# A graph network on one core: a reordered attention loop, and zeros written in an earlier stage

## The chip, the core and the metric

The kernel runs on one core of a Trainium2 chip. The metric is device time in microseconds. The core has a matrix engine (PE, with its weight loads shown as PEld), a vector engine (DVE), an activation engine (ACT), a general engine (POOL, which also starts the indirect DMAs), and SP, whose queue starts the plain DMAs. The engines run side by side and meet only in semaphores.

## What is computed

Four layers over a graph of 3125 nodes with 128 features and 103125 edges, sorted by destination. Before each layer x is normalized and passed through a relu, and each layer's result is added to x.

```python
edge_index = jnp.stack([src, dst])
x = x + gcn(relu(layernorm(x)), edge_index)          # counts of edges and degrees, two linear steps, softmax
x = x + additive_attention(relu(layernorm(x)))       # 4 heads: exp(tanh(xs + xd) . att), weighted sums
x = x + gat(relu(layernorm(x)))                      # 2 heads, below
x = x + interaction(relu(layernorm(x)), edge_attr)   # below

# gat
xl = (h @ Wl + bl).reshape(n, H, D); xr = (h @ Wr + br).reshape(n, H, D)
e = leaky_relu(xl[src] + xr[dst], 0.2)
alpha = segment_softmax(einsum('ehd,hd->eh', e, att), dst)
out = segment_sum(xl[src] * alpha[..., None], dst).mean(axis=1)

# interaction
msg = (rbf @ k2f_W) * (xa @ Wj + bj)[idx_j]
xj = segment_sum(msg, idx_i)                         # idx_i = src: not sorted
```

## The kernel before

The edges are cut into 202 tiles of 512 (four blocks of 128). Since they are sorted by destination, the destinations of a tile lie in a window of 20 nodes. The kernel is a chain of stages. Each stage is a block in which every engine has a program of its own, and the next stage begins when all engines are through.

**The degree count** (`count_degrees`, L769 on, stage "deg") comes early, in the first layer. DVE writes the two digits of each destination as one-hot rows, 101 steps of two instructions (L790), PE counts with them, ACT and DVE make the inverse root, and SP stores the result and loads it back in two forms (L842 to L848). POOL has nothing to do in it.

**The attention loops** (`attend`, L1321 on) serve both the additive layer and the GAT layer (`gat` is true). `over_tiles` writes out, for each engine, the order of its steps in one period, each step with a lag: `(3, scores)` means that in the period of tile s the scores of tile s-3 are made. A step's waits are semaphores counted by tile. For one period of the GAT loop, PE runs:

- `scores` (L1412, L1415): a matmul with the one-hots and four passes with the activated features, into bank 4, which has no second buffer;
- `turn_sums` (L1457): turns the sums of tile s-5, two transposes, into bank 7. It waits for ACT's `copy_sums` and until `best` holds all tiles up to s-4, since the best scores lie in bank 7 too;
- `features` (L1399, L1403): eight transposes of gathered rows and two matmuls with the window of the destinations;
- `sums` (L1443): eight passes over the gathered rows with the edge weights, into bank 6. It waits for `edge_weights`, and it is what releases POOL's next `gather` into the same slot, six tiles on;
- `turn` (L1424): four transposes of the exponentials; `turn_top` (L1434): the best scores per node into bank 7.

DVE runs `tops` (largest score, L1521 to L1528), `keep_sums` (L1548, takes turned sums out of bank 7), `onehots` (L1158), `leaky` (L1514), `edge_weights` (L1535, takes the turned exponentials out of bank 5) and `best_of_nodes` (L1541, L1544, reads bank 7). ACT runs `raise_scores` (the exponential, L1482), `activate` (L1474 in the GAT loop, L1476 in the additive one) and a copy of the sums (L1488, in the additive loop `keep_sums`, L1494). POOL gathers four blocks of source rows per tile (L744). SP loads indices, local rows and windows.

In the additive loop PE runs scores, features, turn, sums; scores and weights have two banks each there.

**The interaction layer** makes messages and adds them to eight tables in DRAM by indirect DMAs with an add (L1309), since its sums aren't sorted. The tables, `k.sums`, have to be zero. This is done in `load_sources` (L2079 on, stage "srcs"), right ahead of the loop's preparation: DVE clears half of `k.wide` and SP writes it to each of the eight tables with two DMAs, a large one and a small one:

```python
for two in k.sums:
    for table in two:
        sp.dma_start(table[0:k.n_nodes, :]..., zeros...).then_inc(zeroed, 16)
        sp.dma_start(table[k.n_nodes:k.n_nodes + P, :], zeros[:, 0:F]).then_inc(zeroed, 16)
```

The stage also loads the sources of all edges and casts them to float (L2094). Of the buffers, `k.fa` is half of `fm_ab`; in the degree count nobody else uses it.

Of the kernel before, what the change touches and what calls it, by code (L numbers as in the profile page):

```python
# [33 lines left out]
P = 128  # L34
F = 128
# [4 lines left out]
SUB = 4  # L40
TILE = P * SUB
RING = 4
DEEP = 6
# [725 lines left out]
def count_degrees(k):  # L769
# [23 lines left out]
    with Stage(k, "deg") as st:  # L793
        step, digits, high_ready, low_ready, counted = (st.sem("step"), st.sem("digits"), st.sem("high_ready"),
                                                        st.sem("low_ready"), st.sem("counted"))
        rooted, inverted, stored, spread = st.sem("rooted"), st.sem("inverted"), st.sem("stored"), st.sem("spread")
        with st.block() as block:
            @block.vector
            def _(dve):
# [39 lines left out]
            @block.sync  # L839
            def _(sp):  # L840
                sp.wait_ge(inverted, 1)
                sp.dma_start(k.isd.rearrange("(h l) -> h l", l=DIGIT), found).then_inc(stored, 16)  # L842
                sp.wait_ge(stored, 16)
                with nc.allow_non_contiguous_dma(reason="one number per node"):
                    sp.dma_start(k.inv_sqrt_deg[:, :], k.isd.rearrange("(o n) -> o n", o=1).to_broadcast(
                        [P, k.n_nodes])).then_inc(spread, 16)
                    sp.dma_start(k.inv_sqrt_deg_nm[:, :], k.isd.rearrange("(b p) -> p b", p=P)).then_inc(spread, 16)
                sp.wait_ge(spread, 32)  # L848


# [470 lines left out]
def attend(k, name, a, table, table_dst):  # L1321
# [33 lines left out]
    with Stage(k, name) as st:  # L1355
# [12 lines left out]
        with st.block() as block:  # L1368
# [20 lines left out]
            def _(pe):  # L1389
# [70 lines left out]
                if gat:  # L1460
                    over_tiles(pe, k.tiles, [(3, scores), (5, turn_sums), (1, features), (4, sums), (3, turn),
                                             (3, turn_top)], head=2, ring=DEEP)
                else:
                    over_tiles(pe, k.tiles, [(2, scores), (1, features), (3, turn), (4, sums)], head=2,
                               ring=DEEP)

            @block.scalar
            def _(act):
# [31 lines left out]
                else:  # L1500
                    over_tiles(act, k.tiles, [(2, raise_scores), (1, activate), (4, keep_sums)], head=2, ring=DEEP)

            @block.vector
            def _(dve):
# [46 lines left out]
                if gat:  # L1551
                    over_tiles(dve, k.tiles, [(3, tops), (5, keep_sums), (0, onehots), (1, leaky),
                                              (3, edge_weights), (3, best_of_nodes)], head=2, ring=DEEP)
                else:
# [524 lines left out]
def load_sources(k):  # L2079
# [4 lines left out]
    k.earlier = k.fb[:, 0:SUB * P].rearrange("p (j e) -> p j e", e=P)  # L2084
    zeros = k.wide[:, 0, :]
    with Stage(k, "srcs") as st:
        loaded, cleared, zeroed = st.sem("loaded"), st.sem("cleared"), st.sem("zeroed")
        with st.block() as block:
            @block.vector
            def _(dve):  # L2090
                dve.memset(zeros, 0.0).then_inc(cleared, 1)
                dve.tensor_scalar(k.spare[:, :], k.iota_p[:, :], float(k.n_nodes), None, ALU.add)
# [3 lines left out]
            @block.sync  # L2096
            def _(sp):
                sp.dma_start(raw, k.ins["src_edges"]).then_inc(loaded, 16)
                sp.wait_ge(cleared, 1)
                for two in k.sums:  # L2100
                    for table in two:
                        sp.dma_start(table[0:k.n_nodes, :].rearrange("(b p) f -> p b f", p=P),
                                     zeros.rearrange("p (b f) -> p b f", f=F)).then_inc(zeroed, 16)
                        sp.dma_start(table[k.n_nodes:k.n_nodes + P, :], zeros[:, 0:F]).then_inc(zeroed, 16)
                sp.wait_ge(loaded, 16)
                sp.wait_ge(zeroed, 32 * 2 * SUB)

# [138 lines left out]
```

## Time and profile before

| | us |
|---|---|
| median of 3 runs | 5661.89 (5657.54 to 5664.57) |
| the profiled execution | 5659.49 |
| its span, first to last instruction | 5657.8 |
| PE busy in the span | 3980.4 (70%) |
| POOL busy | 3127.6 (55%) |
| DVE busy | 2796.4 (49%) |
| ACT busy | 1440.7 (25%) |

The rows further down come from one profiled execution. Times are microseconds from the start of its span unless marked ns. An engine's busy time is the time in which it had an instruction running; the ends of matmuls are modelled, so that rows of PE are best read from start to start. The granted clock of PE is given in parts of 2.4 GHz. The DMA share is how busy the 16 DMA engines were on average. A row of the windows gives the stretch, its length, the busy time of each engine with its count of instructions, the granted clock, the DMA share and the GB/s. In brackets behind a row of a timeline stands how long its engine had been idle before, and what ended that; "issue" means that the profile shows nothing that it waited for.

### The profile page before, as it was taken

How to read it: one execution, taken by the hardware profiler on the slowest of the kernel's cores; microseconds unless marked ns; L12 is line 12 of the kernel's file. 1: busy time of each engine (PE TensorE's matmuls, PEld its weight loads, DVE VectorE, ACT ScalarE, POOL GpSimd, SP SyncE). 2: the span in 40 equal slices, each digit the busy share in tenths (PEclk: the TensorE clock that was granted, in tenths of full speed). 3: DMA queues.
4: the chain of work that ended last, by engine and by line, in shares of the span. 5: the costliest groups of instructions: out<-in, count | busy, mean ns of one | idle time of the engine just before them, and what ended most of it. 6: DMA issues, size and time to landing. Idle time of an engine off the chain costs nothing. (4 is left out here: it accounts for less than half of the span.)

```text
span 5657.8 us, 85234 instructions
## 1 busy us (share of the span) xinstructions
PE 3980.4 (70%) x18200; PEld 2339.9 (41%) x18200; DVE 2796.4 (49%) x7514; ACT 1440.7 (25%) x3414; POOL 3127.6 (55%) x3371
## 2 busy tenths in 40 slices
PE   3499564989888724999999999326666566656525
PEld 2233333555545412444444444015555555545401
DVE  7799123333333354555555555544444444444447
ACT  0233102333333212333333333011111111111125
POOL 0061123777777522555555554406888888888810
PEclk9999786887888756999999999565555555555557
DMA  1122332222222103333333332045566666666540
GB/s 31 34 67 88 97 96 69 69 70 69 69 69 69 41 0 97 99 97 97 98 97 97 97 97 75 1 114 100 94 96 97 95 97 96 97 96 96 88 100 12
DMA packets 515411, 447.78 MB, mean 79 GB/s; under 512 B 175623, under 2 KB 430678, under 8 KB 515030
## 3 DMA queue, kind: packets, MB, share of 16 engines
q0 software_dynamic: 180992, 211.97, 20.7%
q1 hardware_dynamic: 334294, 234.52, 15.2%
q14 instruction: 92, 0.75, 0.0%
q8 instruction: 33, 0.54, 0.0%
HBM read 336.65 MB, written 109.55 MB: 79 GB/s over the span
## 5 line engine op out<-in xcount | busy, mean ns | idle before, releaser
L1309 POOL DMA_INDIRECT sums<-gathered,idx x808 | 1307.3, 1618 | 419.0 <-issue 228.3
L744 POOL DMA_INDIRECT gathered<-table,idx x1088 | 1028.8, 946 | 796.8 <-DMA idx<-in_src_rows 285.2
L1415 PE MATMUL bank<-zact,att_cells 128*64 128x512 f32 (+1 forms) x1212 | 683.4, 676 | 0.9 <-ACT zact L1476 0.5
L744 POOL DMA_INDIRECT wide<-table,idx x528 | 498.8, 945 | 250.9 <-issue 135.7
L1235 PE MATMUL bank<-msg,gathered 128*128 128x128 f32 x1616 | 418.9, 441 | 262.6 <-DVE msg L1277 262.6
L1521 DVE TENSOR_REDUCE neg_raw<-bank 80x1 f32<-80x512 f32 (+1 forms) x404 | 276.5, 684 | 608.0 <-PE bank L1415 608.0
L1482 ACT ACTIVATE msg<-bank,neg_top 80x512 f32<-80x512 f32 (+1 forms) x404 | 275.9, 683 | 1121.2 <-DVE neg_top L1523 1116.2
L978 POOL TENSOR_TENSOR acc<-acc,msg 128x20 f32 x404 | 176.4, 437 | 617.9 <-issue 397.0
L1235 PEld LDWEIGHTS bank<-msg,gathered 128*128 128x128 f32 x1616 | 360.0, 328 | 315.7 <-DVE msg L1277 161.5
L1295 DVE TENSOR_TENSOR idx<-picked,partial 128x4 int32<-128x4 f32 x202 | 33.2, 164 | 803.3 <-DMA sums<-gathered,idx 802.3
L1217 PE MATMUL bank<-w_L_gnn_k2f_W,edge_rows 64*128 64x128 f32 x1616 | 418.9, 438 | 10.2 <-DMA edge_rows<-in_attr_rows 10.2
L1251 ACT COPY gathered<-bank 128x512 f32<-128x512 f32 x202 | 118.4, 586 | 1108.7 <-DMA sums<-gathered,idx 1101.4
L1217 PEld LDWEIGHTS bank<-w_L_gnn_k2f_W,edge_rows 64*128 64x128 f32 x1616 | 359.6, 325 | 55.6 <-issue 44.7
L1399 PE MATMUL bank<-ident,gathered 128*128 128x128 f32 x1632 | 292.1, 304 | 100.2 <-DMA gathered<-table,idx 98.8
L1225 PE MATMUL bank<-window,onehot_t 60*128 60x128 bf16 x808 | 121.3, 303 | 325.0 <-DVE onehot_t L1158 321.0
L1535 DVE COPY edge_rows<-bank 128x320 f32<-128x320 f32 (+1 forms) x404 | 185.2, 458 | 324.1 <-PE bank L1424 323.9
L1514 DVE TENSOR_TENSOR zact<-zact,bank 128x512 f32<-128x512 f32 x404 | 259.7, 684 | 149.4 <-ACT zact L1474 149.4
L1399 PEld LDWEIGHTS bank<-ident,gathered 128*128 128x128 f32 x1632 | 208.8, 152 | 266.4 <-issue 135.4
L927 DVE TENSOR_SCALAR gathered<-iota_c,partial 128x500 f16<-128x500 f16 x812 | 304.7, 391 | 3.3 <-issue 1.6
L1158 DVE TENSOR_SCALAR onehot_t<-dst_row,iota_w,always 64x512 bf16<-64x512 bf16 x606 | 264.5, 436 | 67.0 <-DMA dst_row<-local_rows 41.8
L1443 PE MATMUL bank<-gathered,edge_rows 128*64 128x256 f32 x1088 | 263.9, 385 | 0.0
L935 PE MATMUL bank<-gathered,zact 128*128 128x500 f16 x812 | 209.7, 381 | 69.9 <-DVE zact L928 59.4
(313 smaller groups left out, 6492.3 us busy)
## 6 DMA issues: line engine op xcount, KB each, us to landing
zact<-in_src_flat SPq DMA_DIRECT2D x202, 256.0 KB, 3.4
dst_row<-local_rows SPq DMA_DIRECT2D x606, 64.0 KB, 2.8
edge_rows<-in_attr_rows SPq DMA_DIRECT2D x202, 128.0 KB
gathered<-table,idx POOLq DMA_INDIRECT x1088, 2.7
sums<-gathered,idx POOLq DMA_INDIRECT x808, 3.5
sums<-wide SPq DMA_DIRECT2D x8, 1600.0 KB
counts<-wide SPq DMA_DIRECT2D x4, 3000.0 KB, 12.1
counts<-fm_ab SPq DMA_DIRECT2D x4, 3000.0 KB, 12.0
```

Of the source, the lines that this page charges most:

```text
L744: pool.indirect_dma_start(out=g[:, j, :], out_offset=None, in_=table, in_offset=bass.IndirectOffsetOnAxis(ap=k.idx[t.slot][:, j:j + 1], ax ...
L927: dve.tensor_scalar(k.cell_hot[slot][:, j, :], k.iota_c[:, :], k.cell[:, q], None, ALU.is_equal)
L1158: return dve.tensor_scalar(k.onehot_t[buf][:, :], k.dst_row[t.slot][:, :], k.iota_w[0:HROWS, 0:1], k.always[0:HROWS, 0:1], ALU.is_equal, A ...
L1217: mm = pe.matmul(k.bank[t.two][:, j * F:(j + 1) * F], k.attr[t.two][0:depth, j * P:(j + 1) * P], k.w["L3_gnn_k2f_W"][:, :], start=True, st ...
L1235: mm = pe.matmul(k.bank[4 + t.two][:, j * F:(j + 1) * F], same(t)[:, j, :], k.msg[t.two][:, j, :], start=True, stop=True)
L1309: pool.indirect_dma_start(out=k.sums[t.two][j], out_offset=bass.IndirectOffsetOnAxis(ap=k.idx[t.slot][:, j:j + 1], axis=0), in_=out_rows(t ...
L1399: pe.matmul(z_bank(t, h)[:, j * P:(j + 1) * P], g[:, j, h * F:(h + 1) * F], k.ident[:, :], is_transpose=True, start=(j == 0), stop=False, ...
L1415: mm = pe.matmul(score_bank(t), a.att[h][:, :], k.zact[t.two][:, h, :], start=False, stop=(h == a.zs - 1))
L1443: mm = pe.matmul(sum_bank(t), weights(t)[:, j, :], g[:, j, :], start=(j == 0), stop=(j == SUB - 1))
L1482: act.activation(raised(t), score_bank(t), ACT.Exp, bias=k.neg_top[0:cells, bass.ds(t.t, 1)], accum_out=k.weight_sum[0:cells, bass.ds(t.t, ...
L1514: m = dve.tensor_tensor(za, za, z_bank(t, h)[:, :], ALU.max)
L1521: dve.tensor_reduce(raw, score_bank(t), AX.X, ALU.max, negate=True).then_inc(top_found, 1)
```

## The change

- In the GAT loop PE's order becomes scores, features, turn_sums, sums, turn_top, turn: turn_sums goes behind features, and turn_top ahead of turn.
- In the GAT loop DVE's order becomes tops, onehots, keep_sums, leaky, best_of_nodes, edge_weights.
- In the additive loop ACT runs activate ahead of raise_scores.
- The zeros of the eight tables are written in the degree count: POOL clears `k.fa`, SP issues the 16 DMAs from there, ahead of its other work in the stage, and waits for them at the stage's end. In "srcs" DVE's memset, the 16 DMAs and their wait are gone.

```diff
@@ count_degrees @@
+        cleared, zeroed = st.sem("cleared"), st.sem("zeroed")
         with st.block() as block:
+            @block.gpsimd
+            def _(pool):
+                pool.memset(k.fa[:, :], 0.0).then_inc(cleared, 1)
...
             @block.sync
             def _(sp):
+                sp.wait_ge(cleared, 1)
+                for two in k.sums:
+                    for table in two:
+                        sp.dma_start(table[0:k.n_nodes, :].rearrange("(b p) f -> p b f", p=P),
+                                     k.fa[:, :].rearrange("p (b f) -> p b f", f=F)).then_inc(zeroed, 16)
+                        sp.dma_start(table[k.n_nodes:k.n_nodes + P, :], k.fa[:, 0:F]).then_inc(zeroed, 16)
                 sp.wait_ge(inverted, 1)
...
                 sp.wait_ge(spread, 32)
+                sp.wait_ge(zeroed, 32 * 2 * SUB)
@@ attend @@
-                    over_tiles(pe, k.tiles, [(3, scores), (5, turn_sums), (1, features), (4, sums), (3, turn),
-                                             (3, turn_top)], head=2, ring=DEEP)
+                    over_tiles(pe, k.tiles, [(3, scores), (1, features), (5, turn_sums), (4, sums), (3, turn_top),
+                                             (3, turn)], head=2, ring=DEEP)
...
-                    over_tiles(act, k.tiles, [(2, raise_scores), (1, activate), (4, keep_sums)], head=2, ring=DEEP)
+                    over_tiles(act, k.tiles, [(1, activate), (2, raise_scores), (4, keep_sums)], head=2, ring=DEEP)
...
-                    over_tiles(dve, k.tiles, [(3, tops), (5, keep_sums), (0, onehots), (1, leaky),
-                                              (3, edge_weights), (3, best_of_nodes)], head=2, ring=DEEP)
+                    over_tiles(dve, k.tiles, [(3, tops), (0, onehots), (5, keep_sums), (1, leaky),
+                                              (3, best_of_nodes), (3, edge_weights)], head=2, ring=DEEP)
@@ load_sources @@
-                dve.memset(zeros, 0.0).then_inc(cleared, 1)
...
-                sp.wait_ge(cleared, 1)
-                for two in k.sums:
-                    for table in two:
-                        sp.dma_start(table[0:k.n_nodes, :].rearrange("(b p) f -> p b f", p=P),
-                                     zeros.rearrange("p (b f) -> p b f", f=F)).then_inc(zeroed, 16)
-                        sp.dma_start(table[k.n_nodes:k.n_nodes + P, :], zeros[:, 0:F]).then_inc(zeroed, 16)
                 sp.wait_ge(loaded, 16)
-                sp.wait_ge(zeroed, 32 * 2 * SUB)
```

## Rows read from the trace of the kernel before

**Rows 1.** Windows, us: busy of PE, PEld, DVE, ACT, POOL; clock, DMA share.

```profile
2230.00:3530.00 1300.00, 1296.73 (x6248) 635.84 (x6249) 711.72 (x2017) 438.34 (x1009) 758.78 (x803) 1.00 0.35 96
945.00:1960.00 1015.00, 894.06 (x3994) 511.61 (x3992) 345.44 (x810) 394.28 (x1403) 742.83 (x786) 0.81 0.27 67
3830.00:5400.00 1570.00, 942.67 (x4040) 788.78 (x4040) 691.78 (x1616) 236.85 (x404) 1306.68 (x808) 0.50 0.60 95
53.00:164.00 111.00, 59.57 (x803) 48.04 (x804) 110.72 (x203) 0.00 (x0) 0.00 (x0) 1.00 0.00 0
3772.00:3818.00 46.00, 0.00 (x0) 0.00 (x0) 0.19 (x1) 0.00 (x0) 0.00 (x0) 0.50 0.94 280
```

**Rows 2.** Groups, additive loop, 1000 to 1900: busy us, mean ns | idle before, releaser.

```profile
L744 POOL DMA_INDIRECT gathered<-table,idx x480 | 453.8, 945 | 146.3 <-issue 131.0 <-PE bank L1447 15.2
```

**Rows 3.** Timeline, PE, one tile of the GAT loop: start, us, operation [idle before].

```profile
2806.64 0.46 PE L1424 MATMUL bank<-ident,msg 64*128 64x64 f32 x4
2807.03 0.20 PE L1434 MATMUL bank<-top_cells,own 64*2 64x20 f32 x2
2807.16 0.40 PE L1412 MATMUL bank<-onehot_t,far 64*64 64x512 bf16 x1
2807.49 1.93 PE L1415 MATMUL bank<-zact,att_cells 128*64 128x512 f32 x4
2809.35 0.33 PE L1457 MATMUL bank<-ident,tile_rows 64*128 64x64 f32 x2
2809.62 1.09 PE L1399 MATMUL bank<-ident,gathered 128*128 128x128 f32 x8
...
2811.17 1.94 PE L1443 MATMUL bank<-wide,edge_rows 128*64 128x256 f32 x8
2813.05 0.46 PE L1424 MATMUL bank<-ident,msg 64*128 64x64 f32 x4
```

**Rows 4.** Timeline of the stage srcs and the two after it, SP's queue and DVE.

```profile
3768.22 0.36 SPq L2098 DMA_DIRECT2D partial<-in_src_edges  x1
...
3771.62 0.57 DVE L2094 CAST partial<-partial 128x808 f32<-128x808 int32 x1
...
3822.08 0.06 DVE L517 MEMSET win_off<- 128x1 f32 x1 [49.89 <-PEq L158]
3822.93 0.33 DVE L429 TENSOR_SCALAR base<-first,win_off 128x202 f32<-128x202 f32 x1 [0.78 <-PEq L158]
```

**Rows 5.** Timeline of setup, POOL: a memset of 128 columns.

```profile
1.68 0.19 POOL L323 MEMSET ones<- 128x128 f32 x1
```

**Rows 6.** Line L1158 in the interaction loop, 3850 to 5300: count, ns min/median/max.

```profile
L1158 DVE TENSOR_SCALAR onehot_t<-dst_row,iota_w,always x190: 395/405/754, 3850.8 to 5296.3; 64x512 bf16<-64x512 bf16 x190
```

**Rows 7.** Timeline, GAT loop, the same tile: DVE and ACT.

```profile
2808.19 0.16 DVE L1544 TENSOR_TENSOR fm_ab<-fm_ab,bank 2x20 f32 x1
...
2810.56 0.68 ACT L1482 ACTIVATE msg<-bank,neg_top 64x512 f32<-64x512 f32 x1 [3.45 <-DVE neg_top L1523]
...
2810.68 0.28 DVE L1548 COPY partial<-bank 128x40 f32 x1
...
2811.91 1.28 DVE L1514 TENSOR_TENSOR zact<-zact,bank 128x512 f32<-128x512 f32 x2 [0.72 <-ACT zact L1474]
```

**Rows 8.** Timeline, PE, end of the GAT loop, where features have run out.

```profile
3520.49 0.33 PE L1457 MATMUL bank<-ident,tile_rows 64*128 64x64 f32 x2
3520.76 1.51 PE L1443 MATMUL bank<-gathered,edge_rows 128*64 128x256 f32 x6
```

**Rows 9.** Groups, GAT loop, 2300 to 3500, weight loads: busy us, mean ns | idle before.

```profile
L1443 PEld LDWEIGHTS bank<-gathered,edge_rows 128*64 128x64 f32 x1001 | 126.8, 136 | 112.2 <-issue 53.0
...
L1399 PEld LDWEIGHTS bank<-ident,gathered 128*128 128x128 f32 x1000 | 106.9, 141 | 8.5
...
L1424 PEld LDWEIGHTS bank<-ident,msg 64*128 64x128 f32 x752 | 60.9, 138 | 72.3 <-issue 72.3
...
L1434 PEld LDWEIGHTS bank<-top_cells,own 64*2 64x2 f32 x376 | 15.7, 79 | 12.7
```

More of the change, by code:

```diff
@@ L2084, in load_sources @@
     k.earlier = k.fb[:, 0:SUB * P].rearrange("p (j e) -> p j e", e=P)
-    zeros = k.wide[:, 0, :]
     with Stage(k, "srcs") as st:
-        loaded, cleared, zeroed = st.sem("loaded"), st.sem("cleared"), st.sem("zeroed")
+        loaded = st.sem("loaded")
         with st.block() as block:
```

## The prediction

> **What bounds the kernel now.** I first cut the span into its stages and read, for each, the busy time of every engine, the granted clock and the share of DMA [rows 1]. Three loops over the 202 tiles carry most of it. In the GAT loop (first row) PE is busy 1296.7 of 1300 us at a granted clock of 1.00, which is its 2.4 GHz level, and no other engine reaches 60%: it is bound by PE. In the additive loop (second row) PE is busy 88% at 0.81, which mixes 1.2 and 2.4 GHz; POOL has 742.8 us of 1015, but the row of its gathers shows that this is full [rows 2]: 945 ns busy and 0.30 us of idle before each (146.3/480), nearly all of it issue, so 1.25 us in all, and 4 x 1.25 = 5.0 us is the whole period of a tile (202 x 5.0 = 1010). That loop is bound by POOL. The interaction loop (third row) has POOL at 83%, with its scatters. The last two rows are stages between loops: while the degrees are counted the DMA queues carry nothing (share 0.00), with DVE busy all through; while the tables are zeroed the DMA share is 0.94 and no engine has work.
>
> Next I read one period of the GAT loop on PE [rows 3]. From start to start: turn 0.39, turn_top 0.13, first matmul of scores 0.33, the rest of scores 1.86, turn_sums 0.27, features 1.55, sums 1.88, together 6.41 us; 202 tiles make 1295 us. There is no idle row in between. Whatever the reorder does to waits can bring nothing here unless the work itself gets shorter.
>
> **Part 1, the zeros.** Removed from the stage "srcs": one memset, 16 DMAs and the wait for them. The stage now issues its load of the sources at 3768.22, casts at 3771.62 and hands over to the next stage at 3822.08 [rows 4]. Left over are the load and the cast. The cast began at 3771.62, so the load had landed by then; it takes 0.57, and from the end of one stage to the first instruction of the next DVE idles 0.78 (last row of the group). So the next stage starts at 3771.62 + 0.57 + 0.78 = 3772.97 instead of 3822.08: **-49.1 us**. Everything behind it is shifted, since the chain there is serial.
>
> Added to the degree count: a memset on POOL and the same 16 DMAs on SP's queue, then a last wait. The 16 transfers ran some 46 us at 280 GB/s [rows 1]; begun with the one-hots at about 54 they end near 100, even at half the rate near 146. The store of the degrees, which they stand in front of in SP's queue, is only due when DVE ends at 164. So they are hidden; uncovered they would cost the 46 us again. What isn't hidden is what they do to DVE, on which this stage hangs. The memset: POOL cleared 128 columns in 0.19 us [rows 5], so 3200 take at most 25 x 0.19 = 4.7 us. DVE's digit operations at the head of the stage run beside it; if they had to wait it out it would cost 4.7, if they don't meet, 0. The nearest row is a DVE tensor_scalar beside POOL's scatters and the busiest DMA of a loop (a share of 0.60) [rows 1, 6]: minimum 395, median 405, maximum 754 ns. The median is 2.5% over the minimum, so I take **+1 us** for memset and the 46 us of traffic together (2.5% of 46 is 1.2), with 0 and 4.7 + 1.2 = 6 as ends.
>
> The Trainium skill ("SBUF — State Buffer", section "SBUF: two separate sides") says that VectorE in a two-port mode and GpSimd take one port pair as an exclusive lock for a whole instruction. By it the digit operations would wait for the whole memset, and the sum would be some 4 us higher; the median of 405 beside POOL doesn't show it, the 754 ns maximum may.
>
> **Part 2, the additive loop.** ACT's activate of a new tile now goes ahead of the exponential of the one before. PE needs the activated tile for the scores of the next period, and the exponential only for turn, behind the next scores and features. Neither touches POOL, which issues without a pause. By the lags in the code PE makes the sums of tile s-4 when it takes the rows of s-1, and POOL waits for the sums six tiles back, so it stands some two tiles before its release. I take **0**. A gain is excluded by the 5.0 us of four gathers; a loss needs PE to fall two periods (10 us) behind.
>
> **Part 3, the GAT loop.** No instruction is added. PE runs scores, features, turn_sums, sums, turn_top, turn. Counting from the start of scores (2807.16) and keeping the lengths above, features starts at 2.19, turn_sums at 3.74, sums at 4.01, turn_top at 5.89, turn at 6.02, the next scores at 6.41. Each wait against that:
> - turn_sums needs the best scores of the tile before; DVE had them at 2808.19 + 0.16, which is 1.19 [rows 7], and gets them earlier now. Spare 2.5 us; before it was 1.0, the tightest of all.
> - turn_top needs keep_sums, 0.28 us on DVE behind turn_sums: 4.01 + 0.28 and an allowance of 0.1 make 4.4, against 5.89. Spare 1.5 us.
> - turn needs the exponential, done at 2810.56 + 0.68, so 4.08, against 6.02. Spare 1.9 us.
> - sums of the next period, at 10.4, needs edge_weights, which now stands behind best_of_nodes: it starts after turn (6.41), waits for at most 0.33 of best_of_nodes and ends before 7.4. Spare 3 us.
> - What is queued behind keep_sums on DVE is leaky; it started at 2811.91 (4.75), after ACT. keep_sums is through at 4.4. Should it come later, leaky has until the scores two periods on.
> - POOL's gathers are released by sums, which ends as before.
>
> So no wait opens, and PE stays full. What is open is whether a stage costs the same behind another neighbour. One new pair happens at the end of the loop already, where the features have run out: turn_sums straight into sums, 0.27 us from start to start [rows 8], as long as turn_sums into features. The other pairs I price from the loads. Bounds: each stage begins with a weight load (79 to 141 ns [rows 9]), and six neighbours change; every stage keeps its own load, so what can change is how much of it shows. I take **0** for the period; the ends are half a load of 138 ns saved a tile, and twice the 54 ns of rival 1 lost: -14 and +22 us. At the very end of the loop best_of_nodes comes before edge_weights, and the last turn_sums waits less: **-1 us**.
>
> **Sum.** The profiled execution took 5659.5 us (5657.8 of span and 1.7 around it), 2.4 below the median of 5661.9. 5659.5 - 49.1 + 1 + 0 + 0 - 1 = 5610.4, and at the median's level **5613 us** (-0.86%).
>
> **Rivals.**
> 1. *Exposed weight loads.* A load is hidden behind a long stage and bare behind a short one. Bare before: those of turn_top and features (79 + 141 ns); bare now: those of turn and sums (138 + 136), with the one of scores bare in both [rows 9]. That is +54 ns a tile, 202 x 0.054 = 11 us: 5624; with twice as much 5635. Against it: before the first load of turn the loader sat idle for 0.38 us a tile (72.3/188), behind the longest stage, so that load isn't pulled ahead and hidden now either. The Trainium skill ("TensorE: Matmul & The Clock Gate", section "Step-by-step: what each phase is for") says that PE pulls weight loads ahead of matmuls in flight; this rival is what that rule gives here.
> 2. *Cheaper neighbours.* The mirror image: turn_top's tiny load (79 ns) now follows the longest stage, and PE saves the 0.07 a tile of the lower end: 5599.
> 3. *The zeros hurt the degree count.* If its DVE work is held by the memset and slowed by traffic past my bound, by 15% over 46 us, it is 7 + 4 us in place of the 1: 5623. For it: no row shows DVE beside a DMA share of 0.94. Against it: the 2.5% at 0.60.
> 4. *Slower: a bubble that takes the clock down.* If PE has to wait in each period, for keep_sums behind turn_sums, it loses the wait and perhaps the 2.4 GHz too: the additive loop, where PE is idle 12% of the time, is granted 0.81. At 0.90 the GAT loop's 1297 us become 1441, 5757 in all. It decides from 0.24 us a tile (49/202). keep_sums would have to be 1.5 us later than I make it before PE waits at all.
> 5. *The zeros aren't taken off the path.* If SP's queue were still full of them when the degrees are due, part of the 49 us comes back in the degree count; the 60 us between 100 and 164 speak against it. With all of it back, 5662.
>
> **Chances.** Forecast (5606 to 5619) 0.58; rival 1 0.18; rival 2 0.11; rival 3 0.06; rival 4 0.04; rival 5 0.03. The range of **5598 to 5634** takes in the first four but for the worst of rival 1. About 0.2% (11 us) is what a measurement of this kernel can tell from no change. Faster by more than that: 0.93; within it: 0.03; slower: 0.04.
>
> **What would show it.** In the profile after, "srcs" should pass from its load to the next stage in about 5 us instead of 54, and the stretch of the degree count should show a DMA share near 0.9 for some 46 us, with DVE's one-hots at 0.54 us each (110.7/203) and the count ending within 1 to 6 us of before. The GAT loop should keep 6.41 us a tile at a clock of 1.00 with no idle time on PE; a period of 6.46 is rival 1, one of 6.34 rival 2, a clock under 1.00 with PE waiting for DVE rival 4. The additive loop should keep its 1.25 us a gather. I'm wrong if PE's period moves by more than 0.1 us, or if the one-hots get longer beside the zeros.

## The result, and the profile after

| | before | after |
|---|---|---|
| median, runs side by side | 5663.23 (5657.54 to 5666.03) | 5589.58 (5584.73 to 5596.26) |
| ratio, 95% interval | | 0.9872 [0.9855, 0.9889] |
| profiled execution / its span | 5659.5 / 5657.8 | 5584.7 / 5583.0 |
| PE busy | 3980.4 | 3953.5 |

The change saves 73.7 us, where 49 were forecast; 5589.6 lies below the range of 5598 to 5634. Lines have moved by 12 or so: of the kernel after, L1424 is the far matmul of scores, L1427 its four passes (here called att), L1411 and L1415 the transposes and the windows of features, L1469 turn_sums, L1455 sums, L1446 turn_top, L1436 turn.

One period of the GAT loop on PE, from the timeline of after (start, us, operation; it answers to rows 3):

```profile
2799.90 0.46 PE L1436 MATMUL bank<-ident,msg 64*128 64x64 f32 x4
2800.29 0.40 PE L1424 MATMUL bank<-onehot_t,far 64*64 64x512 bf16 x1
2800.62 1.93 PE L1427 MATMUL bank<-zact,att_cells 128*64 128x512 f32 x4
2802.48 1.09 PE L1411 MATMUL bank<-ident,gathered 128*128 128x128 f32 x8
2803.51 0.60 PE L1415 MATMUL bank<-onehot_t,window 60*128 60x512 bf16 x2
2803.95 0.28 PE L1469 MATMUL bank<-ident,tile_rows 64*128 64x64 f32 x2
2804.16 1.94 PE L1455 MATMUL bank<-wide,edge_rows 128*64 128x256 f32 x8
2806.03 0.20 PE L1446 MATMUL bank<-top_cells,own 64*2 64x20 f32 x2
2806.16 0.46 PE L1436 MATMUL bank<-ident,msg 64*128 64x64 f32 x4
```

The period is 2806.16 - 2799.90 = 6.26 us, where it was 6.41. Counted over some 1060 us it is 6.262 (169 tiles), before 6.407 (166 tiles). The same 30 instructions run, and two stretches of them are shorter. From start to start, the windows take 0.44 us, and turn_sums 0.21 (0.26 to 0.27 before). The windows took 0.53 before, as this row, the one left out of rows 3, shows (timeline of before; sums starts at 2804.77):

```profile
2804.24 0.60 PE L1403 MATMUL bank<-onehot_t,window 60*128 60x512 bf16 x2
2804.77 1.94 PE L1443 MATMUL bank<-gathered,edge_rows 128*64 128x256 f32 x8
```

All others are as long as they were [rows 3]. What happened between the two shows in the weight loads. First before, then after, in the timelines of PEld; in brackets stands how long the loader had been idle:

```profile
2809.35 0.20 PEld L1457 LDWEIGHTS bank<-ident,tile_rows 64*128 64x128 f32 x2 [0.81 <-issue]
...
2811.17 1.05 PEld L1443 LDWEIGHTS bank<-wide,edge_rows 128*64 128x64 f32 x6 [0.42 <-issue]
```

```profile
2802.48 0.86 PEld L1411 LDWEIGHTS bank<-ident,gathered 128*128 128x128 f32 x8 [0.81 <-issue]
2803.50 0.11 PEld L1415 LDWEIGHTS bank<-onehot_t,window 60*128 60x128 bf16 x2 [0.16 <-issue]
2803.73 0.35 PEld L1469 LDWEIGHTS bank<-ident,tile_rows 64*128 64x128 f32 x2
2804.15 1.49 PEld L1455 LDWEIGHTS bank<-wide,edge_rows 128*64 128x64 f32 x8
```

Set each load's start beside that of its first matmul. Before, the load of turn_sums starts at 2809.35 and so does its matmul [rows 3]: the load lies bare. After, it starts at 2803.73 and its matmul at 2803.95, while the second matmul of the windows is still running: it is hidden. Every other first load of a stage is bare in both kernels: taken as means from 2400 to 3360 us, all eight of before start 0.002 to 0.004 us ahead of their matmul, and so do seven of after, while the one of turn_sums starts 0.214 ahead. The two stretches together are 0.145 us shorter, about one load (0.137 us), and 202 times that is the 29 us.

The stages, as windows (stretch, length, busy of PE, PEld, DVE, ACT, POOL; clock, DMA share, GB/s), answering to rows 1:

```profile
2230.00:3500.00 1270.00, 1264.98 (x6227) 650.60 (x6228) 721.88 (x2009) 423.37 (x1006) 762.90 (x808) 0.99 0.36 99
945.00:1960.00 1015.00, 889.50 (x4005) 509.99 (x4005) 348.02 (x813) 384.67 (x1407) 744.38 (x789) 0.82 0.27 67
53.00:104.00 51.00, 25.57 (x344) 20.60 (x344) 50.86 (x94) 0.00 (x0) 0.00 (x0) 1.00 0.95 267
104.00:164.00 60.00, 32.70 (x440) 26.39 (x441) 60.00 (x112) 0.00 (x0) 0.00 (x0) 1.00 0.00 0
```

PE is still full in the GAT loop and the additive loop is as it was. The last two rows show the zeros: DMA share 0.95 up to 104, then nothing, with DVE full in both. The head of the degree count, in the timelines of DVE and POOL after:

```profile
50.17 3.15 DVE L806 TENSOR_SCALAR wide<-dst_f 128x808 f32<-128x808 f32 x1 [0.70 <-PEq L158]
...
50.13 2.76 POOL L801 MEMSET fm_ab<- 128x3200 f32 x1 [42.31 <-POOLq L158]
```

DVE's first digit operation takes 3.15 us beside POOL's memset; the same operation took 0.58 before:

```profile
50.46 0.58 DVE L801 TENSOR_SCALAR wide<-dst_f 128x808 f32<-128x808 f32 x1 [0.70 <-PEq L158]
```

And the stage srcs, with the two behind it (timeline of SP's queue and DVE, answering to rows 4):

```profile
3744.14 0.37 SPq L2108 DMA_DIRECT2D partial<-in_src_edges  x1
...
3747.39 0.58 DVE L2104 CAST partial<-partial 128x808 f32<-128x808 int32 x1 [3.04 <-DMA partial<-in_src_edges]
...
3749.55 0.33 DVE L429 TENSOR_SCALAR base<-first,win_off 128x202 f32<-128x202 f32 x1 [0.78 <-PEq L158]
```

**Where the 74.8 us between the two profiled executions are.** The first transpose of the GAT loop comes at 2226.43 before and 2231.98 after: +5.5. SP's store of the degrees went from 165.44 to 167.73, so 2.3 of that is the degree count. The other 3.2 is no more than executions differ by at that point: it came at 2232.95 in a kernel whose only edit lies behind it (e3). From that transpose to the last turn_sums: 1305.6 to 1276.2, **-29.4**. From there to the stage srcs: -0.2. From the load of the sources to L429: 54.7 to 5.4, **-49.3**. Behind that: -1.4.

### The profile page after: what moved, and what is told of

It is laid out like the page before. It is cut to its first block and busy times, and to the rows that moved or that the text cites. A ratio compares the mean times of both kernels' runs of the same rounds, so it can differ in the third digit from the quotient of the medians.

```text
span 5583.0 us, 85234 instructions
## 1 busy us (share of the span) xinstructions
PE 3953.5 (71%) x18200; PEld 2357.2 (42%) x18200; DVE 2813.4 (50%) x7513; ACT 1415.3 (25%) x3414; POOL 3128.9 (56%) x3372
## 5 line engine op out<-in xcount | busy, mean ns | idle before, releaser
L1427 PE MATMUL bank<-zact,att_cells 128*64 128x512 f32 (+1 forms) x1212 | 680.7, 673 | 0.5 <-ACT zact L1488 0.5
L1411 PE MATMUL bank<-ident,gathered 128*128 128x128 f32 x1632 | 292.6, 302 | 102.6 <-DMA gathered<-table,idx 100.8
L1411 PEld LDWEIGHTS bank<-ident,gathered 128*128 128x128 f32 x1632 | 208.4, 151 | 366.8 <-issue 240.1
L939 DVE TENSOR_SCALAR gathered<-iota_c,partial 128x500 f16<-128x500 f16 x812 | 275.3, 339 | 5.2 <-PE bank L947 2.0
L1488 ACT ACTIVATE zact<-bank 128x512 f32<-128x512 f32 x202 | 120.6, 597 | 570.4 <-PE bank L1415 570.4
L1455 PE MATMUL bank<-gathered,edge_rows 128*64 128x256 f32 x1088 | 263.9, 385 | 0.0
```

Of the source, the lines that this page charges most:

```text
L939: dve.tensor_scalar(k.cell_hot[slot][:, j, :], k.iota_c[:, :], k.cell[:, q], None, ALU.is_equal)
L1411: pe.matmul(z_bank(t, h)[:, j * P:(j + 1) * P], g[:, j, h * F:(h + 1) * F], k.ident[:, :], is_transpose=True, start=(j == 0), stop=False, ...
L1427: mm = pe.matmul(score_bank(t), a.att[h][:, :], k.zact[t.two][:, h, :], start=False, stop=(h == a.zs - 1))
L1455: mm = pe.matmul(sum_bank(t), weights(t)[:, j, :], g[:, j, :], start=(j == 0), stop=(j == SUB - 1))
```

## The experiments

**Theory A.** The chip runs PE in modes by the shape of the stationary tile, which the profile shows as rows*columns: 64*128, 128*64 and so on (60*128 would be of the class 64*128, 64*2 of its own). Where the next stage's class is another, PE drains, and the next load can't be pulled ahead. The order before had a change at all eight borders; the order after has seven, since the windows (60*128) and turn_sums (64*128) now touch. The Trainium skill ("TensorEngine Tiling (Array Packing)", section "Key Properties") says "Changing tiling mode (not just tile) drains the TensorE". It gives no price; the rows above put 0.14 to 0.15 us to one. What the rows show is where each load starts; they don't show that PE drains. **Rivals**: the gain comes from turn_top's new place (C), or from turn_sums standing behind the features whatever the shapes (B). In the expectations of e1 and e2 the letter B stands for other rivals, which are answered there.

**e1: the zeros alone.** The kernel after, with PE's, DVE's and ACT's orders of before.

> The zeros are written in the degree count, and the three reorders are undone. The trace of the changed kernel has the first digit operation of DVE at 3.15 us instead of 0.58 beside POOL's memset and the stage srcs 49.5 us shorter. Theory A (the rest of the gain, some 27 us, comes from PE's order in the GAT loop): -49 + 2.6 = -46, about 5617, ratio 0.992, GAT loop at 6.41 us a tile. Theory B (the zeros give more than that, for example because something later runs better): below 5605.

5621.16 us, ratio 0.9928 [0.9911, 0.9945]; the GAT tile takes 6.407 us. The zeros are worth 44 us (31 to 50 by the interval), which agrees with -49.3 + 2.3 from the trace. That they give more than that (B there) falls: the time is well above 5605.

**e2: turn_sums alone.** The kernel before, with one pair exchanged:

```diff
-                    over_tiles(pe, k.tiles, [(3, scores), (5, turn_sums), (1, features), (4, sums), (3, turn),
+                    over_tiles(pe, k.tiles, [(3, scores), (1, features), (5, turn_sums), (4, sums), (3, turn),
```

> The kernel before with one edit: PE makes turn_sums behind features. DVE's order, turn and turn_top stay. Theory A (PE drains when the shape of the stationary tile changes, in classes of 64 or 128 rows and 32, 64 or 128 columns; windows and turn_sums are both 64 rows by 128 columns, so one switch of eight goes): 6.26 us a tile, -30 us, about 5633, ratio 0.9947. Theory B (a wait went, and DVE's new order is needed for it): 6.41 a tile, 5663. Theory C (a load is bare behind a short stage): 6.41 or more.

5633.37 us, 0.9951 [0.9935, 0.9968]: -31.5, and 6.260 us a tile. That is the whole gain of the loop, with DVE's order of before, so it wasn't a wait that needed DVE's new order (B there).

**e3: turn_top alone.** The kernel before, with turn_top ahead of turn on PE and best_of_nodes ahead of edge_weights on DVE.

> The kernel before with turn_top ahead of turn on PE and best_of_nodes ahead of edge_weights on DVE, nothing else. Theory A (shape classes): turn_top is 64 by 32, turn 64 by 128, their neighbours 128 by 64 and 64 by 64, so each of the three borders is a switch in either order: 6.41 a tile, within 3 us of before. Theory C (the small load of turn_top behind the longest stage saves): 6.34, -14 us, ratio 0.9975.

5664.84 us, 1.0001 [0.9992, 1.0011], 6.407 us a tile. Rival C falls. The three parts sum to 43.7 + 31.5 + 0.1 = 75.3 us; the change gives 73.7, so the new order of ACT in the additive loop, which none of the three has, is left with nothing measurable.

**e4: a border made equal by padding.** The kernel before; the stationary tile of turn_top is padded from 2 to 64 columns, so that it has the class of the far matmul behind it:

```diff
-        self.own = k.sb(f"own{layer}", [self.cells, F if layer == 1 else heads])
+        self.own_wide = k.sb(f"own{layer}", [self.cells, F if layer == 1 else 64])
...
-                    pe.matmul(top_bank(t), a.own[:, :], k.top_cells[t.two][:, :], start=True,
+                    pe.matmul(k.bank[7][0:64, 256:256 + WIN], a.own_wide[:, :], k.top_cells[t.two][:, :], start=True,
```

> The kernel before, its order untouched, with the stationary tile of turn_top widened from 2 to 64 columns by zeros (more work: two longer loads a tile). Theory A (shape classes): turn_top becomes 64 by 64, as the first matmul of scores behind it, and one switch goes: 6.27 to 6.30 us a tile, -22 to -30 us, about 5637. Theory C (loads cost by their length): 6.41 plus 0.05 or more, 5673 or more.

5659.73 us, 0.9992 [0.9983, 1.0002], 6.393 us a tile (6.407 before). The trace gives 3 us; the interval of the total takes in 0. A expected at least 22. The timelines of PEld and PE:

```profile
2804.13 0.19 PEld L1436 LDWEIGHTS bank<-top_cells,own 64*64 64x64 f32 x2
2804.24 0.11 PEld L1414 LDWEIGHTS bank<-onehot_t,far 64*64 64x64 bf16 x1
...
2804.13 0.29 PE L1436 MATMUL bank<-top_cells,own 64*64 64x20 f32 x2
2804.27 0.38 PE L1414 MATMUL bank<-onehot_t,far 64*64 64x512 bf16 x1
```

The load of far does start early (2804.24 against 2804.27), but by 0.03 us: turn_top streams 20 columns, and there is little to hide behind. The padding also made each of turn_top's own two loads longer, from 79 to 131 ns. So there are two explanations after the fact, a short matmul ahead and dearer loads, and this run doesn't separate them; e6 and e7 below bear on both.

**e5: the border made unequal again.** The kernel after; turn_sums' two transposes take rows 0 to 31 only, which makes their tile 32*128. The sums of the second head are left out.

```diff
-                        mm = pe.transpose(turned_bank(t)[:, h * cells:(h + 1) * cells],
-                                          k.tile_rows[t.two][:, h * F:(h + 1) * F], k.ident[0:cells, 0:cells])
+                        r = slice(0, stride)
+                        mm = pe.transpose(turned_bank(t)[:, h * (cells + stride):h * (cells + stride) + stride],
+                                          k.tile_rows[t.two][r, h * F:(h + 1) * F], k.ident[r, r])
```

> The kernel after, in which the two transposes of turn_sums take only rows 0 to 31 of tile_rows (stationary tile 32*128 where it was 64*128). The sums of the second head are therefore left out of the output: rows 32 to 63 are never turned. Work per tile falls (two transposes stream 32 rows of identity instead of 64). Theory A (PE drains, and can pull no weight load ahead, where the shape class of the stationary tile changes): the border windows to turn_sums is a change of class again, so the load that was hidden (about 0.15 us) lies open again, and the GAT tile takes 6.35 to 6.40 us instead of 6.26, less up to 0.05 for the shorter transposes: 5589 + 202 x (0.05 to 0.13) = 5600 to 5615 us. Rival B (the gain came from the place alone: whatever stands behind the features has its load pulled ahead; the classes don't matter): the load stays hidden and the shorter transposes give up to 0.05 us a tile: 5579 to 5590 us.

5610.66 us, 0.9905 [0.9889, 0.9922], 6.380 us a tile: less work, and 22 us more than e8 below, which is the kernel after but for a memset and ran beside it. The timeline of PEld:

```profile
2802.67 0.11 PEld L1415 LDWEIGHTS bank<-onehot_t,window 60*128 60x128 bf16 x2 [0.17 <-issue]
2803.21 0.20 PEld L1470 LDWEIGHTS bank<-ident,tile_rows 32*128 32x128 f32 x2 [0.42 <-issue]
```

The order is that of after; only the shape of the two transposes changed (and where the second writes), and the load is bare again, with the loader idle for 0.42 us ahead of it. Rival B falls.

**e6: the order grouped by shape.** The kernel after with the same instructions in another order, scores cut into far and near (the four passes of att), DVE and ACT ordered to suit:

```diff
-                    over_tiles(pe, k.tiles, [(3, scores), (1, features), (5, turn_sums), (4, sums), (3, turn_top),
-                                             (3, turn)], head=2, ring=DEEP)
+                    over_tiles(pe, k.tiles, [(3, far), (4, turn_top), (3, near), (4, sums), (1, features),
+                                             (5, turn_sums), (3, turn)], head=2, ring=DEEP)
...
-                    over_tiles(act, k.tiles, [(3, raise_scores), (1, activate), (4, copy_sums)], head=2, ring=DEEP)
+                    over_tiles(act, k.tiles, [(3, raise_scores), (4, copy_sums), (1, activate)], head=2, ring=DEEP)
...
-                    over_tiles(dve, k.tiles, [(3, tops), (0, onehots), (5, keep_sums), (1, leaky),
-                                              (3, best_of_nodes), (3, edge_weights)], head=2, ring=DEEP)
+                    over_tiles(dve, k.tiles, [(4, best_of_nodes), (3, tops), (0, onehots), (5, keep_sums),
+                                              (3, edge_weights), (1, leaky)], head=2, ring=DEEP)
```

> The kernel after with the same instructions in another order: on PE far (tile t-3), turn_top (4), att (3), sums (4), features (1), turn_sums (5), turn (3), with DVE's and ScalarE's orders to suit. Theory A: the class of the stationary tile changes 5 times a tile instead of 7 (att and sums are both 128*64, windows, turn_sums and turn all 64*128), so two more loads of 0.14 to 0.15 us can be pulled ahead, and the drains between them go too: 5.95 to 6.1 us a tile instead of 6.26, 5589 - 202 x (0.16 to 0.31) = 5526 to 5557 us. Rival B (the gain came from the place of turn_sums alone): 6.26 us stays, 5589 +- 3. Rival D: the new order makes PE wait for DVE or ScalarE (att waits for ScalarE's activate, turn for raise): a stall of PE shows in the waits and the tile takes 6.3 us or more, 5600 or more.

5543.24 us, 0.9791 [0.9774, 0.9807], 6.039 us a tile. The changes of class went from seven to five and the tile lost 0.223 us, 0.112 for each. The forecast held. The border from turn_sums to turn, timelines of PEld and PE:

```profile
2803.74 0.32 PEld L1453 LDWEIGHTS bank<-ident,msg 64*128 64x128 f32 x4
...
2803.79 0.41 PE L1453 MATMUL bank<-ident,msg 64*128 64x64 f32 x4
2804.13 0.40 PE L1439 MATMUL bank<-onehot_t,far 64*64 64x512 bf16 x1
```

From start to start and as means over the loop, att and sums take 3.59 us where they took 3.73 in after, and turn_sums and turn 0.46 where they took 0.60: 0.145 and 0.139 less, one load each. The load of turn has a lead of only 0.055 us, and nearly a whole load is saved all the same, so the lead doesn't measure the gain. The stretch from far to the next stage grew from 0.330 to 0.394, since turn_top's wait is met late there; that takes 0.06 back.

**e7 and e11: two classes.** e6, with the stationary tiles of far, att, sums and turn_top padded to 72 columns; the added columns write rows that nobody reads (two of the changed lines).

```diff
+        self.wide = max(self.cells, 72)
...
-        self.far = k.sb(f"far{layer}", [HROWS, self.cells], BF16)
+        self.far_wide = k.sb(f"far{layer}", [HROWS, self.wide], BF16)
```

> The run before this one (grouped order), and the stationary tiles of far, att, sums and turn_top padded to 72 columns, which makes them 64*128 or 128*128: two classes, two changes a tile. The padded columns write rows that nobody reads. The matmuls stream as many columns as before. Theory A: three more loads can be pulled ahead: 202 x 3 x 0.14 = 85 us less than the run before, if loads of 72 columns take no longer than those of 64; if they take as long as those of 128 (0.14 against 0.13), some 0.1 us a tile of that is given back: 5.5 to 5.75 us a tile, 5440 to 5500 us. From e4 (a padded turn_top gave 0.02 us, since its own matmul is too short to hide the next load) I take the upper half as likelier. POOL's gathers, 5.0 us a tile, are the floor below which PE's savings show nothing. Rival B: 0 against the run before, or slower by the longer loads (+0.05 us a tile, +10).

5527.83 us, 0.9762 [0.9745, 0.9778], and 5.960 us a tile; A had expected 5.5 to 5.75. The same kernel again, beside e12:

> e7's kernel once more, so that e9's can be set beside it in one and the same call: e9 and e10 ran on a chip on which the kernel before takes 5961 us, not 5662, and on which DVE and ScalarE stand still for some microseconds every 25 to 30 us in the additive loop too, which no edit touches. On a chip where before takes 5662: 5.96 us a tile and 5528 us, as in e7. On a chip like that of e9, Theory A: between before's 5961 and e9's 6030.

5528.10 us, 0.9760 [0.9743, 0.9776], 5.959 us a tile. Its timelines of PE and PEld:

```profile
2805.32 0.38 PE L1444 MATMUL bank<-onehot_t,far 64*72 64x512 bf16 x1
2805.84 0.27 PE L1468 MATMUL bank<-top_cells,own 64*72 64x20 f32 x2
2806.04 1.08 PE L1449 MATMUL bank<-zact,att_cells 128*72 128x512 f32 x2
...
2803.32 1.01 PEld L1421 LDWEIGHTS bank<-ident,wide 128*128 128x128 f32 x8
2805.26 0.12 PEld L1444 LDWEIGHTS bank<-onehot_t,far 64*72 64x72 bf16 x1
2805.81 0.20 PEld L1468 LDWEIGHTS bank<-top_cells,own 64*72 64x72 f32 x2 [0.43 <-issue]
```

Padding to 72 does put 128*72 with 128*128: the load of the transposes starts at 2803.32, 0.22 ahead of its matmul (2803.54). The border from sums to the transposes gave 0.155 us and turn 0.09. But from far to turn_top 0.52 us pass here (0.48 in the mean, 0.39 in e6), though the two are of one class, and turn_top itself, ahead of a change of class in both kernels, takes 0.203 us where it took 0.132. That 0.07 is the price of padding its two loads. The group of turn_top in e7 named an idle PE ahead of it (busy, mean ns | idle before):

```profile
L1468 PE MATMUL bank<-top_cells,own 64*72 64x20 f32 x388 | 52.9, 212 | 19.2 <-issue 0.2
```

In the code turn_top waits for keep_sums of the tile that turn_sums has just turned, as both use bank 7. If a load stands behind its own instruction's wait, PE pays the wait and the load; e9 was made to test that.

The 0.07 also bears on e4. An estimate from it and from the lengths of the loads (79 ns, 131 in e4, 138 here) puts the padding of e4 at 0.06 us, so the equal border there gave some 0.08 against the 0.014 that was left: about half of what the others gave, behind the shortest matmul.

**e9 and e12: the wait met early.** e7, with turn_sums 0.44 us earlier, between transposes and windows, which `features` is cut into:

```diff
                     over_tiles(pe, k.tiles, [(3, far), (4, turn_top), (3, near), (4, sums), (1, features),
-                                             (5, turn_sums), (3, turn)], head=2, ring=DEEP)
+                                             (5, turn_sums), (1, windows), (3, turn)], head=2, ring=DEEP)
```

> e7 with one move: turn_sums of tile t-5 stands between the 8 transposes of the gathered rows and the 2 windows' matmuls, where it stood behind the windows. In e7 (5.96 us a tile instead of the 5.5 to 5.75 expected) PE waited before turn_top, 19.2 us in 195 tiles, until DVE had kept the sums that turn_sums had just turned, and its load (0.14) started only then, though far and turn_top are of one class. Theory A (that wait is what e7 missed): with turn_sums 0.44 us earlier the wait is met, the load of turn_top hides behind far's 0.21 us, and the tile takes 5.75 to 5.86 us, 5527.8 - 202 x (0.10 to 0.21) = 5485 to 5508 us. Rival F (the load of turn_top lies open for another reason, the change from bf16 to fp32 or rows of another tile): the wait may go, but the load stays, 0.1 us a tile at most: 5508 to 5528. Rival G (turn_sums now waits for ScalarE's copy, which ends 0.2 us before): slower than e7.

e9 and e10 (below) ran on a chip of which the others tell nothing: there the kernel before takes 5961.15 us, and e9 takes 6030.37, 1.0119 [1.0102, 1.0136]. The timeline of e9 shows what is different there:

```profile
3272.20 1.09 ACT L1513 ACTIVATE zact<-bank 128x512 f32<-128x512 f32 x2 [4.30 <-remote]
3272.25 0.20 DVE L1587 COPY partial<-bank 128x40 f32 x1 [4.85 <-remote]
...
3272.71 0.40 PE L1472 MATMUL bank<-top_cells,own 64*72 64x20 f32 x2 [3.21 <-issue]
3273.03 3.69 PE L1453 MATMUL bank<-zact,att_cells 128*72 128x512 f32 x4
```

ACT and DVE stand still together for over 4 us, with a releaser that the profile can only call remote, 28 times each in 800 us of this loop. PE runs out of work, and its next four passes take 3.69 us instead of 1.94: the granted clock over them is 0.50, the lower level. In the additive loop, which e9 shares with e7, one line of DVE alone loses 167.7 us in 32 such waits within 600 us, and in e7 none. The kernel before is 5% slower there as well. So this is that chip's, not e9's; but e9 loses more by it than before does. e12 is e9's kernel once more, beside e11:

> e9's kernel once more. On an undisturbed chip, Theory A (the load of turn_top hides behind far where the wait is met): 5.72 us a tile, which is what e10's trace shows where its clock is full (windows at 3299.67 and 3305.38), so 202 x 0.24 = 48 us less than the run before this one: 5480 us. Rival G (turn_sums between the transposes and the windows makes PE wait, for ScalarE's copy or, later, at turn_top, and the clock falls behind each wait): slower than the run before this one by up to 1%, on an undisturbed chip too: 5530 to 5590 us.

**5485.15 us** (5478.35 to 5485.45), 0.9682 [0.9666, 0.9698], 5.713 us a tile, where 5.72 and 5480 us were forecast. PE and PEld:

```profile
2803.31 0.34 PE L1496 MATMUL bank<-ident,tile_rows 64*128 64x64 f32 x2
2803.48 0.59 PE L1429 MATMUL bank<-onehot_t,window 60*128 60x512 bf16 x2
...
2804.16 0.38 PE L1448 MATMUL bank<-onehot_t,far 64*72 64x512 bf16 x1
2804.38 0.24 PE L1472 MATMUL bank<-top_cells,own 64*72 64x20 f32 x2
2804.55 1.94 PE L1453 MATMUL bank<-zact,att_cells 128*72 128x512 f32 x4
...
2804.19 0.33 PEld L1472 LDWEIGHTS bank<-top_cells,own 64*72 64x72 f32 x2
```

The load of turn_top starts 0.19 us ahead of its matmul, behind far, and far to turn_top takes 0.22 instead of 0.52. So the wait was what e7 had missed. That the load lies open because bf16 gives way to fp32 there (rival F) falls, and so does a new wait of PE behind turn_sums (rival G). Against before the changes of class fell from eight to two and the tile from 6.407 to 5.713: 0.116 us for each of six, with the price of the padding in it.

How far ahead a load starts at an equal border goes with the last matmul ahead of it: 0.03 us behind 20 columns (e4), 0.055 to 0.06 behind fp32 transposes of 64 (e6, e7, e12), 0.21 behind 256 columns in fp32 (e7) or 512 in bf16 (after), 0.43 behind 512 in fp32 (e6). The 0.03 alone proves little: turn_top's load has it too behind its wait in e7 and e9, and in e6 at a change of class.

**e8 and e10: the memset out of the way.** The kernel after (e8) and e9's (e10), with POOL waiting for DVE's digits:

```diff
+                pool.wait_ge(digits, 2)
                 pool.memset(k.fa[:, :], 0.0).then_inc(cleared, 1)
```

> The kernel after, with POOL's memset of fa waiting for the digit operations of DVE, so that it runs beside the one-hots' comparisons and not beside the first digit operation. Theory L (POOL's memset held DVE's first operation by the port that the two share: 3.15 us instead of 0.58): the operation takes 0.58 us again; the memset's 2.8 us fall beside one-hot comparisons that either wait (as L: 0 to 2.6 us later in the same stage) or don't share the port in that form. 5587 to 5590 us. Rival (the 2.6 us are a start-up cost of DVE's instruction, not POOL's memset): it stays at 3.15 us, 5590 us.

5588.20 us, 0.9874 [0.9857, 0.9890]: the total can't tell it from after, the trace can (DVE and POOL):

```profile
50.78 0.58 DVE L807 TENSOR_SCALAR wide<-dst_f 128x808 f32<-128x808 f32 x1 [0.70 <-PEq L158]
...
54.16 12.05 DVE L790 TENSOR_TENSOR gathered<-acc,iota_d 128x400 bf16<-128x400 bf16 x22
...
54.18 2.77 POOL L802 MEMSET fm_ab<- 128x3200 f32 x1 [46.36 <-DVE acc L815]
```

The digit operation is at 0.58 us again, so the 3.15 weren't a start-up cost of DVE's, and SP's store of the degrees comes at 165.76 instead of 167.73. The memset now runs beside the one-hots and costs them nothing: 12.05/22 = 0.548 us each, 0.545 in after, where it doesn't meet them (10.36/19).

> The run before this one, and POOL's memset of fa waiting for DVE's digits as in e8. Theory L and A together: 2.6 us less than the run before, both within what three rounds can tell apart; first digit operation at 0.58 us, the same period of the GAT tile as the run before.

6035.67 us on the chip of e9, a ratio of 1.0119 [1.0102, 1.0136]; it can't be told from e9 there. Between two stalls its GAT tile took 5.72 us, from which e12's forecast was made.

## Why the prediction was right or wrong

- **What bounds the kernel: right.** PE is full in the GAT loop in every kernel here but on the chip of e9, and each gain there was work or bare loads taken from PE.
- **Zeros off the path: right**, -49.3 for -49.1. The 16 transfers ended by 104 at a share of 0.95, and DVE's one-hots kept their pace: from the first start to the last 109.3 us, 109.2 before. Rival 5 had no part, and rival 3 was wrong on the traffic.
- **Memset and traffic at +1: mis-sized.** The trace has +2.3 to the end of the degree count and +2.57 for the first digit operation; all of it is the memset, none the traffic. The ends of 0 and 6 held. The memset itself took 2.76 us, not 4.7. The step taken wrongly was to price a meeting with POOL's memset by the median of an instruction beside scatters [rows 6], which is mostly not meeting it. The Trainium skill's rule of an exclusive lock ("SBUF — State Buffer", section "SBUF: two separate sides"), which the prediction set aside, was the better guide: DVE waited for nearly the whole memset. Its exception shows too: by that section a DVE operation with two inputs in SBUF is held only against a GpSimd operation that reads SBUF; the one-hots, beside a memset that only writes, lost nothing (e8).
- **Additive loop at 0: right.** POOL's gathers keep 1.25 us each ((454.3 + 146.6)/481).
- **Waits of the GAT loop: right.** None opened; PE has no wait in the profile between 2320 and 3380, and the clock is 0.99, so rival 4 had no part.
- **GAT period at 0, ends -14 and +22: wrong, and this is what put the time outside the range.** It was -0.145 us a tile, -29 us. The prediction said that what can change is how much of a load shows, and then bounded that by half a load with no row behind the half. A whole load was the natural end: 202 x 0.138 = 28. The trace held the rule. In rows 3 every stage but the windows, which are left out there, shows its tile, no two neighbours alike; in rows 9 the loader idles 0.38 us ahead of turn, behind the longest stage. The prediction took from this only that "that load isn't pulled ahead", and didn't ask why. Asking could have led to 128*64 beside 64*128, and to the one border in the new order where the tiles agree. It had also noted that turn_sums into sums is as long at the end of the loop as turn_sums into features [rows 8], which is true and concerns the wrong side: the gain was at the border ahead of turn_sums.
- **Rival 2 had the sign and about half the size, with the wrong place.** It gave the gain to turn_top behind sums; e3 shows that to be 0, as each of those borders is a change of shape in either order. Rival 1 was wrong by the same reading: e3 has its neighbours of turn, turn_top and scores and costs nothing. Its premise, that only short stages leave the next load bare, fails in before already, where all eight loads are bare, those behind the 1.87 us of sums and the 1.86 of att too.
- **Loop end at -1:** can't be told; 202 x 0.145 = 29.3 of the loop's 29.4 us leave nothing for it.
- **Open:** whether PE drains where the shape changes or only holds the load back; no row tells these apart. How much of e4's small gain goes to the short matmul and how much to the padding, beyond the estimate above. What stops DVE and ACT on the chip of e9, and why e9 loses 1.2% to before there while it gains 3.2% elsewhere. Neither the kernel after nor e7 was run on it, so a gain of theirs on such a chip isn't shown.

## What to carry to other kernels

In a loop that PE bounds, write down the tile shape (rows*columns) of each stage and count the borders at which it changes; then order the stages so that equal shapes touch, and see whether a few padded columns make more of them equal. Compare the start of each load with that of its first matmul: level starts mean a bare load. In these runs an equal border saved about a load, roughly half of that where the matmul ahead had 20 columns, and little where a wait was met late. So keep a wait's producer early, and count what padding adds to the loads themselves.

## What the runs showed that was not expected

- Where the shape of PE's stationary tile changes, the next load starts with its own matmul and not ahead of it: 0.11 to 0.15 us a tile for each change (e2 0.147, e6 0.112, e12 0.116; the last two with a late wait or with padding in them). That 64*72 goes with 64*128 and 128*72 with 128*128 is shown by e7 and e12 (leads of 0.06 and 0.21 us), that 32*128 doesn't go with 60*128 by e5.
- A DVE tensor_scalar in fp32 took 3.15 us instead of 0.58 beside a POOL memset of 2.76 us; a bf16 comparison of two tensors took 0.55 us with and without it, and with the DMA queues at a share of 0.95.
- One chip ran the kernel before 5% slower than the others (5961 us for 5663) and e9's 10% (6030 for 5485). In e9's trace DVE and ACT stand still for up to 8 us at a time.
